# Cross-attention loops of a two-layer decoder: values of two key tiles in one go, three buffers of exponentials, values read in place and 17 columns wide

## The reference, cut to what matters

```python
def _L0_xattn_ref(q, k, v, mask, wq, bq, wk, bk, wv, bv, wo, bo):   # q from x, k = v = ctx_1024 (2, 1024, 256)
    qh = _split_heads(q @ wq.T + bq, B)
    kh = _split_heads(k @ wk.T + bk, B)
    vh = _split_heads(v @ wv.T + bv, B)
    scores = jnp.einsum('bhqd,bhkd->bhqk', qh, kh) / math.sqrt(D_K)
    scores = jnp.where(mask == 0, jnp.float32(-1000000000.0), scores)
    attn = jax.nn.softmax(scores, axis=-1)
    out = jnp.einsum('bhqk,bhkd->bhqd', attn, vh)
    out = out.transpose(0, 2, 1, 3).reshape(B, -1, D_MODEL)
    return out @ wo.T + bo

def _L1_xattn_ref(q, kv, Wq, Wkv, Wc):
    qp = jnp.einsum('bld,ed->ble', q, Wq)
    idx = jnp.argmax(jnp.einsum('bld,bmd->blm', qp, kv), axis=-1)
    mem = jnp.take_along_axis(kv, idx[..., None], axis=1)            # 512 rows, one per query
    mk, mv = jnp.split(jnp.einsum('bld,ed->ble', mem, Wkv), 2, axis=-1)   # one head of keys and values
    ...                                                              # 16 query heads, softmax, @ Wc.T
```

## Time and profile before

| | us |
|---|---|
| median of three runs | 1187.73 |
| profiled execution | 1187.39 |
| its span | 1185.6 |
| first attention, first score to last values | 218.07 to 434.30 |
| second attention, first score to last values | 876.61 to 1012.2 |
| PE busy over the span | 943.2 (80%) |
| DVE busy | 668.0 (56%) |
| ACT busy | 455.2 (38%) |
| POOL busy | 307.0 (26%) |

### The profile page before, as it was taken

The page is one execution under the profiler, slowest core; times in us unless marked ns, Lnnn a source line. Parts: engine busy times, 40 slices in busy tenths (PEclk is TensorE's granted clock), DMA queues, the critical chain, the costliest instruction groups (busy, mean ns, idle before and its releaser), DMA issues. The chain is left out here.

```text
span 1185.6 us, 13004 instructions
## 1 busy us (share of the span) xinstructions
PE 943.2 (80%) x4000; PEld 472.9 (40%) x4005; DVE 668.0 (56%) x1347; ACT 455.2 (38%) x900; POOL 307.0 (26%) x294
## 2 busy tenths in 40 slices
PE   6879677699999985996489999894958888636985
PEld 3435434123333245664345555453412223412554
DVE  5845585698999633121354445444667885323534
ACT  3775132067777740111143233321206666202321
POOL 7144654000000002001254444454210000065014
PEclk9989988589999996799699999997968999858998
DMA  6000047434535005112540000000321110342000
GB/s 197 1 1 1 18 143 187 115 89 120 151 104 165 6 1 199 50 61 63 205 180 1 1 1 1 1 0 23 73 48 46 39 40 1 137 157 83 27 9 27
DMA packets 45279, 82.13 MB, mean 69 GB/s; under 512 B 9881, under 2 KB 31433, under 8 KB 43273
## 3 DMA queue, kind: packets, MB, share of 16 engines
q1 hardware_dynamic: 42081, 75.55, 21.2%
q0 software_dynamic: 2176, 5.38, 1.3%
q10 hardware_dynamic: 960, 0.43, 0.1%
HBM read 60.08 MB, written 16.54 MB: 65 GB/s over the span
## 5 line engine op out<-in xcount | busy, mean ns | idle before, releaser
L1050 DVE TENSOR_REDUCE c_amx<-PS 128x1 f32<-128x512 f32 x256 | 158.4, 682 | 28.3 <-PE PS L961 28.0
L1141 ACT ACTIVATE c_aE<-PS 128x512 f32<-128x512 f32 x256 | 132.6, 603 | 44.8 <-PE PS L973 44.5
L1599 POOL TENSOR_SCALAR s_Pn<-s_Pr,s_rs 128x512 f32<-128x512 f32 x64 | 99.9, 1563 | 123.0 <-DVE s_rs L1626 122.8
L961 PE MATMUL PS<-c_aKs,c_aQs 99*128 99x512 bf16 x256 | 106.5, 419 | 19.5 <-DMA c_aQs<-c_q_stack 18.6
L67 POOL TENSOR_SCALAR rstd<-mv 128x4 f32<-128x4 f32 x10 | 2.3, 232 | 388.0 <-DVE mv L90 387.3
L1617 DVE TENSOR_REDUCE s_mx<-PS 128x1 f32<-128x512 f32 x64 | 44.2, 691 | 100.3 <-PE PS L1730 100.3
L973 PE MATMUL PS<-c_aQs,c_aKs 99*128 99x512 bf16 x256 | 95.8, 385 | 3.4 <-ACT c_aE L1141 2.3
L1683 ACT ACTIVATE s_Pr<-PS,s_nmx 128x512 f32<-128x512 f32 x64 | 44.0, 687 | 137.4 <-DVE s_nmx L1619 137.4
L1050 DVE TENSOR_REDUCE h_amx<-PS 128x1 f32<-128x512 f32 x128 | 79.8, 684 | 26.7 <-PE PS L961 26.5
L1748 PE MATMUL PS<-s_PT,s_V 128*128 128x512 f32 x128 | 67.1, 606 | 18.6 <-DVE s_PT L1633 18.2
L1141 ACT ACTIVATE h_aE<-PS 128x512 f32<-128x512 f32 x128 | 66.9, 603 | 33.5 <-PE PS L973 33.3
(11 more groups left out here) (372 smaller groups left out, 1718.2 us busy)
## 6 DMA issues: line engine op xcount, KB each, us to landing
area<-in_e_w SPq DMA_DIRECT2D x16, 512.0 KB, 9.1
area<-in_g_w SPq DMA_DIRECT2D x8, 1024.0 KB, 17.0
c_aVs<-c_VB SPq DMA_DIRECT2D x8, 512.0 KB, 16.5
g_B<-in_g_b SPq DMA_DIRECT2D x1, 4096.0 KB, 11.6
c_k_stack<-area SPq DMA_DIRECT2D x12, 256.0 KB, 4.6
c_aKs<-c_k_stack SPq DMA_DIRECT2D x8, 384.0 KB
area<-in_ctxT SPq DMA_DIRECT2D x2, 1024.0 KB, 10.0
c_q_stack<-area SPq DMA_DIRECT2D x16, 128.0 KB, 2.5
```

The costliest lines, as they stand in the source:

```text
L961: pe.matmul(PS[:, n % MB, :], self.Qs[u % 3][:, j, qt * P:(qt + 1) * P], self.Ks[u % 3][:, j % self.KH, half * BANK:(half + 1) * BANK], st ...
L1050: dve.tensor_reduce(self.mx[:, qt, j, half:half + 1], PS[:, n % MB, :], AX.X, ALU.max).then_inc(self.max_done, 1)
L1141: act.activation(self.E[kt % 2][:, j, :], PS[:, MB + x % XB, :], ACT.Exp, scale=0.25).then_inc(self.exp_done, 1)
L1599: pool.tensor_scalar(Pn[g % NPB][:, :], Pr[g % NPB][:, :], rs[:, g % NPB:g % NPB + 1], None, ALU.mult).then_inc(pn_ready, 1)
```

## The change

Values are issued for two tiles together, after the steps with even kt: those of the two tiles before. The first step of a unit issues the values of the last two tiles of the unit before. Three buffers of exponentials take the place of two, and the exponentials of tile n wait for the values of tile n - 3. The value products take their weights from VB itself, so Vs, its DMAs and its semaphores go, and TensorE waits for the projection's own semaphore in the first value product of each unit. VB has 17 columns in the place of 32, 16 of values and one of ones. The tile of maxima (MT) keeps its 32.

```diff
-VW = 32
+VW = HD + 1
+MW = 32
...
-        self.Vs = [sb(f"Vs{n}", [P, NK // P, KH, VW]) for n in range(3)]
-        self.E = [sb(f"E{n}", [P, GH, S]) for n in range(2)]
+        self.E = [sb(f"E{n}", [P, GH, S]) for n in range(3)]
...
             if kt == 0:
-                pe.wait_ge(self.v_loaded[u % 3], (u // 3 + 1) * 16)
+                self.wait_values(pe, u // NG)
                 if u > 0:
                     pe.wait_ge(self.o_copied, u)
             pe.wait_ge(self.exp_done, (u * KT + kt + 1) * GH)
             for j in range(GH):
-                last = pe.matmul(PS[32 * j:32 * j + 32, 6, :], self.Vs[u % 3][:, kt, j % self.KH, :],
-                                 self.E[kt % 2][:, j, :], start=(kt == 0), stop=(kt == KT - 1),
+                last = pe.matmul(PS[32 * j:32 * j + VW, 6, :], self.V[:, u, kt, j % self.KH, :],
+                                 self.E[(u * KT + kt) % 3][:, j, :], start=(kt == 0), stop=(kt == KT - 1),
                                  skip_group_check=True)
...
-                if kt > 0:
-                    values(u, kt - 1)
-                elif u > 0:
-                    values(u - 1, KT - 1)
+                if kt % 2 == 0 and u * KT + kt > 0:
+                    for n in range(u * KT + kt - 2, u * KT + kt):
+                        values(*divmod(n, KT))
...
-        values(UNITS - 1, KT - 1)
+        for kt in range(KT - 2, KT):
+            values(UNITS - 1, kt)
...
-                    if n >= 2 and j == 0:
-                        act.wait_ge(self.av_done, n - 1)
-                    act.activation(self.E[kt % 2][:, j, :], PS[:, MB + x % XB, :],
+                    if n >= 3 and j == 0:
+                        act.wait_ge(self.av_done, n - 2)
+                    act.activation(self.E[n % 3][:, j, :], PS[:, MB + x % XB, :],
...
-        sp.dma_start(at.Vs[buf][:, :, :, :],
-                     values[:, bass.ds(u, 1), :, :, :].rearrange("p u t h c -> p (u t) h c")).then_inc(at.v_loaded[buf], 16)
...
+    at.V = VB
+    at.wait_values = lambda pe, b: pe.wait_ge(proj_taken, (b + 1) * NV // B)
...
+    at.V = VB
+    at.wait_values = lambda pe, b: pe.wait_ge(v_ready, b + 1)
```

More of the change, by code:

```diff
@@ L911, in __init__ @@
         self.Ks = [sb(f"Ks{n}", [ROWS, KH, NK], BF16) for n in range(3)]
-        self.Vs = [sb(f"Vs{n}", [P, NK // P, KH, VW]) for n in range(3)]
         self.qtail = sb("qtail", [TAIL_ROWS, GH * S], BF16)
-        self.E = [sb(f"E{n}", [P, GH, S]) for n in range(2)]
+        self.E = [sb(f"E{n}", [P, GH, S]) for n in range(3)]
         self.mx = sb("mx", [P, TB, GH, 2])
         self.m = sb("m", [P, TB, GH])
-        self.MT = sb("MT", [P, TB, GH, VW], BF16)
+        self.MT = sb("MT", [P, TB, GH, MW], BF16)
         self.Oraw = sb("Oraw", [P, S])
@@ L921, in __init__ @@
         self.loaded = [sem(f"loaded{n}") for n in range(3)]
-        self.v_loaded = [sem(f"v_loaded{n}") for n in range(3)]
         (self.s_done, self.max_done, self.m_ready, self.mT_done, self.q_ready,
@@ L1084, in normalise @@
                 self.Otok[:, u, :, :].rearrange("p t (j c) -> p (t j) c", j=GH),
-                PS[:, 7, :].rearrange("p (t c) -> p t c", c=VW)[:, :, 0:HD],
+                PS[:, 7, :].rearrange("p (t c) -> p t c", c=MW)[:, :, 0:HD],
                 self.rc[:, :, :].rearrange("p t j -> p (t j)").unsqueeze(2).to_broadcast([P, TB * GH, HD]),
@@ L1215, in store_parts, with load_unit @@
             sp.dma_start(dst, src).then_inc(done, 16)
-def load_unit(sp, at, q_stack, k_stack, values):
+def load_unit(sp, at, q_stack, k_stack):
     def load(u, buf):
@@ L1423, in _ @@
             weights = sh.weights[0]
-            at.sync(sp, load_unit(sp, at, q_stack, k_stack, VB), rest, also=lambda u: weights.load_expert(sp, u))
+            at.sync(sp, load_unit(sp, at, q_stack, k_stack), rest, also=lambda u: weights.load_expert(sp, u))
             for e in range(2):
@@ L1911, in _ @@
             sp.wait_ge(v_ready, 1)
-            at.sync(sp, load_unit(sp, at, q_stack, k_stack, VB), rest)
+            at.sync(sp, load_unit(sp, at, q_stack, k_stack), rest)
         @block.gpsimd
```

## The result

The changed kernel took 1207.62 us in the median of four runs (1203.11 to 1208.56), the kernel before 1187.54 beside it. The ratio is 1.0147 with a 95% interval of 1.0085 to 1.021: slower, though this interval alone doesn't clear 1%. Run again later, unaltered, it took 1205.12 (1199.19 to 1208.64, six runs), ratio 1.0148 (1.011 to 1.0186), so slower by more than 1%.

What follows compares the result with a forecast made beforehand. TensorE (PE) was taken as the bound, always busy in the first attention, VectorE with hardly any slack. From 1187.4, +6.7 +1.5 -1.6 -2.5 +4.8 -0.8 -1.4 +1.4 = +8.1 gave 1195.5, say 1196; range 1180 to 1208.

Steps and rivals of the forecast that it cites:

- Pairs (6.02): First attention: two steps with values issued together take 6.02 us, set by VectorE, where PE alone would need 5.48.
- The unit's end (+0.73): Step 7 and the next unit's step 0: no values cover the tails' copies any more, 6.17 becomes 6.90, +0.73.
- The eighth unit (+1.5): First attention's eighth unit, without scores: ScalarE is the limit, +0.46 four times, a little hidden by the projection, +1.5.
- 17 columns (-2.4): Value weight loads, only a group's first exposed: 0.05 saved per group, -1.6 in the first attention, -0.8 in the second.
- Values in place (-2.5): Start of the first attention: without the value transfers the first queries land earlier, half of 5.1 taken, -2.5.
- GpSimd (-1.0 in the first attention): Settings of ones fall to one column each, beside the normalisation: -1.0 in the first attention, -0.4 in the second.
- Second attention without the clock (+4.0): Second attention: +4.8 from load-bound units lengthened by 0.73 and its last units, -0.8 from the columns.
- The clock (+1.4): Second attention: PE idles more, so its clock falls to 0.50 in one more unit, +1.4.
- my own mark: Sign that the forecast is wrong: PE's clock at 0.50 at more than three unit ends.
- the clock rival: Second attention: the clock falls at every unit's end, 4 more falls than forecast, 1204 us; chance 0.24.
- Vector rival: Pairs in the attentions: VectorE keeps up, pairs take 5.5, -8.3 stays, 1173 us in all; chance 0.12.
- side-by-side rival: Value passes: the four 17-column products no longer run side by side, +79, 1275 us; chance 0.04.

Runs made afterwards that it cites:

- the second profile: The changed kernel run again later, unaltered: median 1205.12 us, ratio 1.0148; the profiled execution was the fastest of six, 1199.19.
- the first profile: The profiled execution of the changed kernel in its first measurement: median 1207.62 us, ratio 1.0147 to the kernel before.

## Why the prediction was right and where it was wrong

**Pairs (6.02): right.** 5.94, set by VectorE; halving its work gives 5.41. **The unit's end (+0.73): right.** Scores to scores 304.61 to 311.62 = 7.01 against 6.90 reckoned; the transposed score waits 1.03 for the tails, where I had put some 0.8, and covering them gives 0.86 back. (Part of the difference is a slip: four exponentials 0.48 apart, the last 0.6 long, from 0.63 on end at 2.67 and not at 2.57; the tails' copies began at 2.73.) The unit came out at 24.84 where 24.96 was reckoned. **The eighth unit (+1.5): too dear.** It was +0.83 where no fall of the clock disturbed it, in the second profile: from its first transposed score to the last value pass 408.76 to 434.84 = 26.08, before 408.46 to 433.71 = 25.25.

**17 columns (-2.4): mis-sized.** Half the columns are not half the load, and PE gains 0.0125 a group, some 0.6 in all. The figure of the Trainium skill ("TensorE: Matmul & The Clock Gate", section LDWEIGHTS (loading the stationary operand)) would, by my estimate from it, have 17 columns take 14 ns, and the trace has 97; but the saving per group that I worked out from it, 0.01, is what was measured. A duration that hardly depends on the size can't be halved with the size.

**Values in place (-2.5): right.** From SP's first load to the first score 19.8 before (198.29 to 218.07), 17.2 to 18.4 in the seven profiles with the values read in place and uncut loads: 1.4 to 2.6 less. The mixed view of it (half one engine's queue, half bytes) hid the larger thing: with the 19 rows cut the same stretch is 9.6 even with the value loads, and 0.3 to 0.5 less without them. The Trainium skill ("DMA: Bandwidth & Descriptors", section Why a DMA increments its semaphore by 16 and not by 1) gives a transfer the largest number of engines up to 16 that divides its rows, so 19 rows get one and 16 rows sixteen; the runs agree, with 10 us at this place. **GpSimd (-1.0 in the first attention):** 0.5 to 1.0, by the transposes behind the normalisation.

**Second attention without the clock (+4.0): right.** The load-bound period was 14.87 to 14.96, reckoned 14.0 + 0.73 = 14.74. The second profile, with much the same time at the lower clock as before, has +4.66 for the whole loop.

**The clock (+1.4): the step that failed.** It asked only whether the load wait would pass 2.0 us, and charged one more fall at 1.4. The wait stayed (1.85 to 2.17), and 1.4 fits the short falls of the kernel before (15.93 and 15.35 against some 14.1). But the wait for the tails, which the forecast itself had put 3 us behind, was not weighed together with the load wait: a fall now lasts 6.8 us or more, and costs 2.8 (17.79, 17.41, 17.81 against 14.87 and 14.94 in the same profile). With four of them the second attention is 9.6 longer than with one. Of the 12.4 between 1195.5 and 1207.87 the second attention holds 8.9 (14.3 against 5.4). By my own mark (more than three unit ends at 0.50) the clock rival came true in that execution and not in the other; its condition, a wait past 2.0 us, decided nothing. The medians of 1207.6 and 1205.1 suggest that most executions are like the first; no trace of them shows it. The 0.30 for slower by over 1% was too low for the same reason.

**What was luck.** The time lies in the range by 0.4 us, and inside it only because the range was drawn wide enough for the clock rival; "same", with 0.61, did not come. The remaining terms agree with the forecast in sum and not singly: in the first profile the start was 4.4 shorter than forecast, wholly by the earlier start of the normalisation (5.1), in which the change has no part, and the first attention 2.3, the middle 1.9 and the rest of the span 3.8 longer.

**Vector rival and side-by-side rival: out**, by 5.94 per pair and by 1.84 from the first value pass to the next score (reckoned 1.92).

## What to carry to other kernels

When work is moved to save a switch of the engine, ask first what it covered where it stood, and whether another engine lets the saving through: here the 0.18 a pair that PE alone would have gained never came (5.94 with VectorE in the way), and the price was the only cover of a 1 us copy. Splitting the last pair gives the cover back, and where neither loads nor VectorE hold the unit, as in the second attention with cut loads, the pairs then pay (12.20 against 13.10). When TensorE's clock already falls behind one wait, a second idle stretch close behind it can be dearer than its own length: here falls lasted at least 6.8 us instead of 3.4 where 1 us of waiting followed. And if a small load lands last with one DMA engine of sixteen busy, mend that before the order of the work: four lines were worth 2% on the kernel before and some 2.6% on the changed one.

## What the runs showed of the hardware

- In the two attentions' loops TensorE's clock fell behind waits of 1.5 us or more for a load, not behind each of them (18 of 40), for 3.4 us where no idle stretch followed and for 6.8 or 10.2 where 1.03 us of one did. It also fell, for 3.4 us, at 6 of the 11 waits of 1.46 for the tails in a last unit. Waits of 1.02 or 1.03 alone brought none. What picks the waits behind which it falls stays open.
- The same transfer of 19 rows, cut into 16 and 3, took 8 to 10 us off the first wait of the first attention and 2 us off each later one, with two DMAs more per unit.
- A load of float weights took 109 ns for 32 columns and 97 for 17.
